# Two recurrent layers of a five-stage network: their layer normalization moved into the block of the recurrence

## The reference, cut to what matters

```
n = (x - mean(x)) / sqrt(var(x) + 1e-5)            # over the 128 features
c = in_c                                           # the same for 1024 tokens
for t in range(4):                                 # 1024 tokens a step
    f = sigmoid(n[t] @ wf + c @ uf + bf)
    i = sigmoid(n[t] @ wi + c @ ui + bi)
    g = tanh(n[t] @ wc + c @ uc + bc)
    c = f * c + i * g
x[t] = x[t] + 0.5 * tanh(n[t] @ wo + c @ uo + bo)  # all t, the last c
```

## Time and profile before

| | us |
|---|---|
| median of 3 runs | 2816.11 |
| lowest, highest run | 2814.51, 2816.17 |
| the profiled execution | 2814.1 |
| its span, first to last instruction | 2812.3 |
| cell0, from the end of the experts' last instruction to its own last addition (2286.58 to 2366.87) | 80.29 |
| cell1, likewise, from the MLP's last addition (2723.48 to 2809.43) | 85.95 |

### The profile page before, as it was taken

One profiled execution on the slowest core, in us unless ns is written; L12 is line 12 of the kernel. 1 busy time (PEld: TensorE's weight loads), 2 busy tenths in 40 slices (PEclk: granted clock), 3 DMA queues, 4 the chain that ended last, 5 costly groups with the idle time before them and its releaser, 6 DMA issues. The chain is left out here.

```text
span 2812.3 us, 36464 instructions
## 1 busy us (share of the span) xinstructions
PE 2633.2 (94%) x11619; PEld 1977.0 (70%) x11619; DVE 2253.9 (80%) x3349; ACT 1829.7 (65%) x3092; POOL 1232.4 (44%) x1265
## 2 busy tenths in 40 slices
PE   7899999997999999999999997999999989788788
PEld 4688888874666666666666664888888866577566
DVE  5777777777999999999999978777787765578545
ACT  3355555556888888888888863555555555466565
POOL 2466667664232323233333312666666650345200
PEclk9999999998999999999999999999999999789899
DMA  2566666644333333333333323466666610100000
GB/s 63 125 140 137 147 140 131 148 99 150 103 101 103 101 105 99 106 98 107 101 104 100 106 71 75 108 147 143 134 147 146 132 42 1 38 8 8 8 8 30
DMA packets 107391, 271.55 MB, mean 97 GB/s; under 512 B 30784, under 2 KB 35648, under 8 KB 107072
## 3 DMA queue, kind: packets, MB, share of 16 engines
q1 hardware_dynamic: 82192, 235.41, 33.8%
q0 software_dynamic: 24576, 33.62, 4.3%
q10 hardware_dynamic: 432, 0.20, 0.0%
HBM read 258.35 MB, written 10.76 MB: 96 GB/s over the span
## 5 line engine op out<-in xcount | busy, mean ns | idle before, releaser
L628 POOL TENSOR_TENSOR moe_experts_lo<-moe_experts_hidden,moe_experts_hi 128x512 fp32r<-128x512 f32 x512 | 660.9, 1291 | 342.2 <-ACT moe_experts_hi L566 342.1
L909 DVE TENSOR_TENSOR heads_e_lo<-heads_e,heads_e_hi 128x1024 fp32r<-128x1024 f32 x512 | 616.2, 1224 | 25.8
L573 ACT ACTIVATE psum<-psum 128x512 f32<-128x512 f32 x512 | 298.0, 582 | 479.4 <-PE psum L90 479.4
L743 POOL DMA_DIRECT2D heads_left<-heads_parts x512 | 306.7, 612 | 670.2 <-PE psum L797 610.6
L849 ACT ACTIVATE heads_e<-psum 128x1024 f32<-128x1024 f32 x512 | 520.0, 1023 | 107.2 <-PE psum L797 107.2
L600 DVE TENSOR_TENSOR moe_experts_weighted<-moe_spread,psum 128x512 f32<-128x512 f32 x512 | 351.1, 686 | 190.7 <-PE psum L90 186.8
L88 PE MATMUL psum<-heads_e_hi,heads_v_lo 128*128 128x512 f32 x1024 | 429.6, 419 | 18.1 <-DVE heads_u L875 18.1
L88 PE MATMUL psum<-moe_n_hi,moe_w_lo 128*128 128x512 f32 x1024 | 400.8, 391 | 6.0 <-PEq L54 6.0
L89 PE MATMUL psum<-heads_e_lo,heads_v_hi 128*128 128x512 f32 x1024 | 404.1, 395 | 0.0
L90 PE MATMUL psum<-heads_e_hi,heads_v_hi 128*128 128x512 f32 x1024 | 400.9, 392 | 0.0
L89 PE MATMUL psum<-moe_n_lo,moe_w_hi 128*128 128x512 f32 x1024 | 400.1, 391 | 0.0
(11 more groups left out here) (412 smaller groups left out, 4314.3 us busy)
## 6 DMA issues: line engine op xcount, KB each, us to landing
moe_spread<-moe_mask SPq DMA_DIRECT2D x128, 1024.0 KB, 10.4
heads_right<-heads_parts SPq DMA_DIRECT2D x512, 64.0 KB
heads_left<-heads_parts POOLq DMA_DIRECT2D x512, 64.0 KB, 2.5
heads_scale<-heads_inverse_copy SPq DMA_DIRECT2D x64, 512.0 KB, 3.7
moe_experts_raw<-in_gate SPq DMA_DIRECT2D x16, 256.0 KB, 11.7
moe_experts_raw<-in_up SPq DMA_DIRECT2D x16, 256.0 KB, 11.7
moe_experts_raw<-in_down SPq DMA_DIRECT2D x16, 256.0 KB, 11.7
heads_parts<-heads_e_hi SPq DMA_DIRECT2D x16, 256.0 KB, 2.4
```

What stands on the lines that cost most here:

```text
L573: act.activation(psum[:, GATE + p % 2, :], psum[:, GATE + p % 2, :], ACT.Silu).then_inc(silu_ready, 1)
L628: pool.tensor_tensor(lo[:, p, :], hidden[:, p % 2, :], f(hi[:, p, :]), ALU.subtract).then_inc(low_ready, 1)
L743: eng.dma_start(f(tile[row:row + 2 * HEAD, h % 2, :]), parts_dram[dims, order:order + 2, at]).then_inc(loaded[h % 2], 16)
L909: dve.tensor_tensor(e_lo[:, s, :], e[:, s % 4, :], f(e_hi[:, s, :]), ALU.subtract).then_inc(low, 1)
```

## The change

The two blocks of `recurrent_layer` become one. A new class `Norm` holds the pieces of the normalization as methods, and the layer calls them at fixed places in each engine's list. The tokens fall into two groups of four chunks. The four variances of a group go into one PSUM bank, and one root of 16 columns and one reciprocal serve them. Group 0 (the tokens of steps 0 and 1) is normalized first. Group 1 (steps 2 and 3) is centered and squared among the products of steps 0 and 1, one chunk at a time; its root, scaling and spreads follow around the cells of step 1. The low parts of chunks 1, 3, 5 and 7 are VectorE's, the others GpSimd's. The weights are loaded and split in another order, `from_input` of step 0 waits for all of them. The semaphores of `Norm` are cleared in a clear of their own when the layer is left, behind the layer's one block.

The core of the diff:

```
+    norm = Norm(nc, ctx, f"{tag}_norm", psum, consts, x, (n_hi[:, :], n_lo[:, :]), groups=((0, 1, 2, 3), (4, 5, 6, 7)),
+                centers=(0, 1, 2, 3, 7, 7, 7, 7), scales=(7, 4, 5, 7, 7, 6, 7, 6), variances=6, vector_lows=(1, 3, 5, 7))
...
+                for c in range(4):
+                    norm.spread(pe, c)
+                pe.wait_ge(split_low, len(splits))
+                from_input(0, 0)
+                pe.wait_ge(norm.scaled_ready, 3)
+                from_input(0, 1)
+                from_cell(0, 0)
+                norm.difference(pe, 4)
+                from_cell(0, 1)
+                norm.variance(pe, 4)
+                norm.difference(pe, 5)
+                from_input(1, 0)
+                norm.variance(pe, 5)
+                norm.difference(pe, 6)
+                from_input(1, 1)
+                norm.variance(pe, 6)
+                norm.difference(pe, 7)
+                norm.variance(pe, 7)
+                from_cell(1, 0)
+                from_cell(1, 1)
+                for c in range(4, 8):
+                    norm.spread(pe, c)
...
+                for c in range(4):
+                    norm.square(act, c)
+                norm.root(act, 0)
+                high(0, 0)
+                high(0, 1)
+                for c in range(4):
+                    norm.high(act, c)
+                gate(0, 0)
...
+                    low(1, half)
+                norm.invert(dve, 1)
+                norm.diagonals(dve, 4)
+                norm.diagonals(dve, 5)
+                for half in range(HALVES):
+                    next_cell(1, half)
+                norm.scale(dve, 4)
+                for half in range(HALVES):
+                    low(2, half)
+                for c in (5, 6, 7):
+                    if c < 7:
+                        norm.diagonals(dve, c + 1)
+                    norm.scale(dve, c)
```

More of the change, by code:

```diff
@@ L974, in _, with from_input @@
[L974 to L978, removed]
+                def from_input(t, half):
+                    c = t * HALVES + half
+                    at = slice(c * BANK, (c + 1) * BANK)
+                    norm.wait_low(pe, c)
+                    after(pe, gates_ready, t * (3 * HALVES) + (half - 1) * 3)
+                    for gate, (wn, _) in enumerate(GATES):
+                        product(pe, psum[:, half * 3 + gate, :], w[wn], (n_hi[:, at], n_lo[:, at]), last=False)
@@ new lines, in from_cell @@
+                def from_cell(t, half):
+                    pe.wait_ge(low_ready, t * HALVES + half + 1)
+                    for gate, (_, un) in enumerate(GATES):
+                        product(pe, psum[:, half * 3 + gate, :], w[un], (c_hi[:, half, :], c_lo[:, half, :]),
+                                first=False).then_inc(sums_ready, 1)
+                norm.difference(pe, 0)
+                norm.difference(pe, 1)
+                norm.variance(pe, 0)
+                norm.difference(pe, 2)
@@ new lines, in _ @@
+                gate(0, 1)
+                norm.square(act, 5)
+                high(1, 0)
+                norm.square(act, 6)
+                high(1, 1)
+                norm.square(act, 7)
+                norm.root(act, 1)
+                for half in range(HALVES):
+                    gate(1, half)
+                high(2, 0)
+                norm.high(act, 4)
+                high(2, 1)
+                for c in range(5, 8):
+                    norm.high(act, c)
+                for t in (2, 3):
@@ L1002, in _ @@
-                        act.copy(c_hi[:, half, :], cell[:, half, :]).then_inc(high_ready, 1)
+                        high(t + 1, half)
                 for n in range(BATCH * HALVES):
@@ L1026, in _ @@
[L1026 removed]
+                        low(t + 1, half)
                 for n in range(BATCH * HALVES):
@@ L1032, in _ @@
                 dve.wait_ge(added, BATCH * HALVES)
+            @block.gpsimd
+            def _(pool):
+                split_weights(pool, raw_loaded, raws, splits, split_high, split_low)
+                for c in range(CHUNKS):
+                    if c not in norm.vector_lows:
+                        norm.low(pool, c)
 def decayed_attention(nc, tag, psum, consts, w, tables, xn, residual):
```

189 lines of the change are left out of this document (157 added, 32 removed).

## The result

The changed kernel takes 2841.87 us in the median of 7 runs (2819.77 to 2852.17); the kernel before took 2814.51 in 7 runs beside it (2803.18 to 2816.17). The ratio is 1.0088, with a 95% interval of 1.0046 to 1.0129. It is slower. (The ratio, with its interval, is not the quotient of the two medians, which is 1.0097.) Built again unchanged and run in two later groups, it gave 1.0079 (1.0050 to 1.0107; median 2829.31) and 1.0060 (1.0041 to 1.0079; 2831.80). The forecast of 2833 on 2816.1 is a ratio of 1.0060.

The account below looks back on a forecast made before the run. TensorE, without a hole in the recurrence, was taken as the bound. cell0 8.7, cell1 6.1 and seams 1.8 made 16.6 on 2814.1, 2830.7; with 2.0 for the median, 2833. Own range 2829 to 2837; 8 in 10, 2822 to 2841.

Parts of the forecast that it names:

- the second rival: Table switches are dear (2838), or the clock falls in thin stretches too; up to 2842 us, chance 0.15.
- the two clock cases: Rivals: clock not lost in the new waits (2826, chance 0.15); dear switches or low clock (up to 2842, chance 0.15).
- Opening, cell0: cell0's normalization up to step 0's products: first product 8.4 us earlier, input products 1.7 us shorter, gain 10.1.
- Opening, cell1: cell1's normalization up to step 0's products: first product 9.8 us earlier, input products 4.1 instead of 7.01, gain 12.7.
- Inside the recurrence: First to last cell product, per layer: chunks 10.4, variance wait 0.8, third-spread wait 5.5, half clock 2.1; together 18.8 us added.
- The clock was not kept: Rival: clock not lost in the new waits, or back at once; 6.8 us less, 2826, chance 0.15.
- The inner work was not hidden: Rival: TensorE takes up group 1's work and wait beside the recurrence's products; fully hidden 2795 us, chance 0.05.
- the last rival: The parts cancel: the openings win some 15 us each, or the third spread's wait does not arise; about 2818, chance 0.08.
- three signs of being wrong: Third spread waits under 2 us; openings win more than 14 us each; stages behind cell0 shift more than cell0 itself.
- the row's price: On ScalarE a table switch costs 1.28 us, as the trace row shows, without the skill's drain of about 1.4.
- The rival by which a switch is dear behind a running queue: Rival on ScalarE: a switch takes longer than 1.29 us; at twice that 5.2 us more, 2838; shares chance 0.15.
- The seams: Two clears in a row at each recurrent layer's end: 0.9 us more, twice, 1.8; possibly nothing at cell1's end.

Follow-up runs that it names:

- first_only: Only cell0 has the changed layer, cell1 is as in the kernel before; 2829.48 us, ratio 1.0092 to the kernel before.
- one_clear: Changed kernel with the normalization's semaphores in the layer's own clear, so one clear at a layer's end; 2830.56 us, ratio 1.0061 to the kernel before.
- before_two_clears: Kernel before with a spare semaphore cleared apart in each recurrent layer, so two clears at its end; 2817.14 us, ratio 1.0013 to the kernel before.
- no_wait: Changed kernel with group 1's spreads split around half 1's cell products, diagonals and scalings of chunks 4 to 6 ahead of new cells; 2821.64 us, ratio 1.0059.

## Why the prediction was right, and where its numbers were off

**Direction and sum: right.** Slower was forecast with 0.86, and 1.0060 as the size; the two repeats gave 1.0079 and 1.0060, the first measurement 1.0088. Its median of 2841.87 is 8.9 us above the 2833 and 0.9 above the range's upper end of 2841. That excess does not stand in the layers that the sum is about, as far as the profiles show (no execution near that median was profiled). So the number of the second rival, up to 2842, was met by luck: neither of its two causes is in the rows. The chances themselves add up to 0.87 for the forecast and the two clock cases, a little more than the 0.86 given for slower.

**Opening, cell0: right.** Forecast 8.4 us earlier, behind some 3.7 of idle, and 1.7 from the full pace: gain 10.1. Measured 8.3 (18.76 for 27.10), 3.44 and 1.67: gain 10.0. The spreads at half clock were right too: from the first spread to the border of the input products 6.4 us pass, forecast 6.2. The wait was a little shorter than forecast, and the first diagonal is part of that: the forecast's 0.97 us of the earlier trace rows lie beside GpSimd's splits, here the first two took 1.28 together.

**Opening, cell1: right.** 9.9 and 2.9, gain 12.9, for the forecast's 9.8, 2.9 and 12.7. What the prediction did not say is what these gains are made of. The four chunks that left the opening are 10.4 us by its own price, as much as cell0's gain of 10.0; they come back inside the recurrence. The hole at the seam, the thing to be won, stayed as a hole ahead of the first spread.

**Inside the recurrence: right in mechanism, 0.8 and 0.9 us too small.** 19.6 and 19.7 for 18.8. By terms: the waits 6.7 for 6.3; half clock behind the wait 1.6 in cell0 and 2.0 in cell1 for 2.1 (from the third spread to the second product 3.73 and 4.00 us instead of 2.1, and 0.1 more behind it in cell1); what is left of the 12.9 and 13.0 us of added busy time, 11.3 and 11.0 for the 10.4 of the four chunks. So the largest miss is the price of the chunks among the products, and it is partly offset by the clock. The variance of chunk 7 waits 0.69 (forecast 0.8). The third spread waits 6.05, forecast 5.5, on the diagonal of chunk 6, behind both new cells, as forecast. VectorE's timeline shows the chain, and why the wait was longer:

```profile
2330.23 0.68 DVE L401 TENSOR_TENSOR cell_norm_normal<-cell_norm_centered,psum 128x512 f32<-128x512 f32 x1
2330.83 0.69 DVE L1199 TENSOR_TENSOR cell_c_lo<-cell_cell,cell_c_hi 128x512 fp32r<-128x512 f32 x1
2332.11 1.33 DVE L1199 TENSOR_TENSOR cell_c_lo<-cell_cell,cell_c_hi 128x512 fp32r<-128x512 f32 x1 [0.60 <-ACT cell_c_hi L1160]
2333.37 0.68 DVE L392 TENSOR_TENSOR cell_norm_diagonal<-identity,cell_norm_inverse 128x512 f32<-128x512 f32 x1
```

The second low part was to cost 0.6 behind a wait of 0.7. It waited 0.60 and took 1.33.

**The rivals.** The clock was not kept (0.54 behind the wait), and it did not stay low in the thin stretches of cell0's opening, where a difference and a variance keep their 0.94 and 0.81 us; in cell1 it did, and the forecast had that in its sum. The inner work was not hidden: TensorE's busy time grew by 12.9. The openings won 10.0 and 12.9, less than the 15 of the last rival. None of the three signs of being wrong came: the third spread waited 6.05 us, both openings won less than 14, and behind cell0 the stage in between shifted by -6.3 for cell0's +9.9.

**Table loads: the row's price holds.** ScalarE's timeline of the changed kernel, between the steps:

```profile
2321.47 1.28 ACT L376 ACT_TABLE_LOAD   x1
2322.76 0.27 ACT L376 ACTIVATE cell_norm_deviation<-psum,eps 128x16 f32<-128x16 f32 x1
2323.05 1.28 ACT L1154 ACT_TABLE_LOAD   x1
2324.35 3.58 ACT L1154 ACTIVATE cell_gates<-psum,vectors 128x512 f32<-128x512 f32 x6
```

The instruction behind each load starts 1.29 and 1.30 us after the load. The rival by which a switch is dear behind a running queue falls: the first load starts as soon as the copy ahead of it is over. The Trainium skill (ScalarE: Activation LUTs, What ACT_TABLE_LOAD costs) adds a drain of about 1.4 us to each switch. No such time stands in these rows, and here the measurement decides.

**The seams: too dear.** Forecast 0.9 each. Measured 0.56 behind cell0 (from the last addition to the next matmul, 1.55 for 0.99) and 0.6 at the end. The failed step was to read a price of 0.9 per clear from two different seams, 1.86 and 0.97; they differ in more than one clear. The changed kernel's own seam:

```profile
2370.50 0.69 DVE L1254 SCALAR_TENSOR_TENSOR x<-cell_h,x 128x512 f32<-128x512 f32 x1 [0.66 <-ACT cell_h L1193]
2372.74 1.53 PE L202 MATMUL psum<-x,center 128*128 128x512 f32 x3 [3.00 <-PEq L54]
```

**What the forecast did not hold: the stage between the layers.** It took an unchanged stage for an unchanged time. Over the profiles it was 346.8 to 364.3 us long with the same instructions, and a start at half clock was seen only behind the changed cell0. That is where the first median's surplus, and `first_only` costing as much as both layers, may come from; it is not shown. It **stays open** what decides the clock there: not the second clear (`one_clear`, `before_two_clears`), and four matmuls more at the end of cell0 did not prevent it. One profile per kernel cannot tell a tendency of six in nine from chance, and the length of the stage did not follow its start.

## What to carry to other kernels

Before work is moved from a filling stage into a steady one, look for a hole on the engine that bounds both: where TensorE is busy for 28.55 of 28.55 us, the moved work costs its full time, and a new dependency between in-order queues can add a wait; behind the wait of 6.05 us there was a stretch of half clock too, behind that of 0.69 there was none. Take the seam's gain alone: here joining the two stages and leaving the order inside each as it was won 7.6 and 7.0 us of the same two layers (0.9964), while the change lost 9.9 and 7.2. And place a step on a queue by who waits for it first: in the changed kernel a diagonal, and in my mended version a low part, stood behind two new cells that nobody needed as soon.

## What the runs showed of the hardware that was not expected

**VectorE slows down beside GpSimd.** The 1.33 us low part above lies beside a GpSimd instruction, by the timeline of the changed kernel:

```profile
2331.64 1.26 POOL L409 TENSOR_TENSOR cell_n_lo<-cell_norm_normal,cell_n_hi 128x512 fp32r<-128x512 f32 x1 [28.33 <-ACT cell_n_hi L382]
```

The VectorE operation before it, of the same form, took 0.69. In `no_wait` the addition of a new cell took 1.56 us beside such a GpSimd operation of 1.59:

```profile
2339.75 1.56 DVE L1211 TENSOR_TENSOR cell_cell<-cell_kept,cell_new 128x512 f32<-128x512 f32 x1
2339.18 1.59 POOL L409 TENSOR_TENSOR cell_n_lo<-cell_norm_normal,cell_n_hi 128x512 fp32r<-128x512 f32 x1 [3.88 <-ACT cell_n_hi L382]
```

A diagonal took 1.46 there for 0.69, beside one of 1.30. VectorE has no idle time from that diagonal to the low part of chunk 5, so the two may hold some 1.6 of the 2.78 us that TensorE waited for it (an estimate: 0.77 and 0.87 above the usual 0.69). All three read two operands from SBUF; operations that read PSUM (L401) kept their 0.68. The Trainium skill (GPSIMD Engine Reference, Specifications) says that the two engines share SBUF interfaces and that VectorE instructions with two SBUF inputs contend; the rows agree, though no run took the GpSimd work away. So the choice of who takes a low part can lengthen the path of a queue it is not on.

**An unchanged kernel's clock differs from run to run.** The changed kernel's 7 runs had mean granted clocks of 0.953 to 0.964 and times of 2852 to 2820 us, and cell1 of the very same code came out at 93.1 and at 88.9 us in two profiles.
